# A four-layer graph network: layer 1's gathers started while layer 0's parts are stored, and its neighbours rearranged

## Chip, cores and metric

One core of a Trainium2 chip runs one program. The metric is the device time of one execution in microseconds. Its engines are TensorE (PE), VectorE (DVE), ScalarE (ACT), GpSimd (POOL) and SyncE (SP), each with an instruction queue of its own; they wait for each other with semaphores.

## The reference

12,500 nodes and 212,500 edges, 128 features. The edges are sorted by target (`dst`). Each of four layers sums over edges, updates the nodes, adds the old value and normalises:

```python
x = _layernorm(x + _L0_gnn_ref(x, W_t, W_u, b_u, src, dst))
x = _layernorm(x + _L1_gnn_ref(x, eps, stack([src, dst])))
x = _layernorm(x + _L2_gnn_ref(x, ew, ew, src, dst, eps, W1, b1, W2, b2))
x = _layernorm(x + _L3_gnn_ref(x, edge_attr, glob, W_e, b_e, eps, W1, b1, W2, b2, src, dst))
# L0: agg = segment_sum((x @ W_t)[dst], src) / deg;  relu(concat(x, agg) @ W_u + b_u)
# L1: agg = segment_sum(norm * x[dst], src);         agg + (1 + eps) * x
#     norm = deg_inv_sqrt[src] * deg_inv_sqrt[dst]
# L2: agg = segment_sum(x[src] * ew, dst);           relu(((1 + eps) * x + agg) @ W1 + b1) @ W2 + b2
# L3: agg = segment_sum(mish(x[src] + edge_attr @ W_e + b_e), dst); a two-layer network on it and glob
```

So layers 0 and 1 gather at the target and sum at the source, while layers 2 and 3 gather at the source and sum at the target.

## The kernel before

**Tiles and supertiles.** 128 nodes are a block (98 blocks), 128 edges a tile (1664 tiles, padding included), 128 tiles a supertile (13). Within a supertile the edges of layers 0 and 1 are sorted by source on the chip. The sums of all nodes stay in `acc`.

**Gathers.** GpSimd fetches a tile's 128 node rows with one indirect DMA into a ring `M` of 64 tiles: `gathers_src` (line 1765, issue on line 1786) in layers 0 and 1, `gathers_dst` (line 1798, issue on line 1821) in layers 2 and 3. In `gathers_src`, 8 gathers are a batch; before each batch beyond the first 8 GpSimd waits for `s_rel`. SyncE counts landed batches up on `s_arr` and releases slots on `s_rel` in `arrivals_src` (line 1832, waits on lines 1845, 1848 and 1851), five batches behind the arrivals. Layer 0 gathers from `in_x`, layer 1 from the table `t1` (the normalised nodes, scaled by the root of the inverse degree), layer 2 from `x2`, layer 3 from `t3`.

**The consumer.** TensorE multiplies one-hot matrices with gathered tiles, in steps; a supertile has 228 steps, in 38 units of 6. Two units are a group (`group_pe`, line 1717): it loads the group's table entries into registers (line 1702, `TENSOR_LOAD`), and for each unit clears two PSUM banks (1709, 1710), multiplies (1730), closes (1714) and yields. VectorE, in `unit_dve` (line 1745), adds the unit to `acc` (1754), yields, makes the one-hot matrices of the unit after the next (1736) and yields; every fourth unit it loads registers as well (1742).

**The sort** of supertile s+2 runs in slices beside layer 0's units of supertile s (`sort`, line 1201; `period` in `run_vector` and `run_tensor`). At each yield of `unit_dve` VectorE does one sort operation, and behind the unit what is left of the slice. TensorE does a slice after each unit. For each of 16 columns c of a supertile there are, in this order: rank matmuls on TensorE (1390, 1391), maxima of the positions on VectorE (1375, in slice `POS_AT`), masks on VectorE (1355, 1361, in slice `MASK_AT`), their scaling on ScalarE (1369), moves on TensorE (1399). Within a slice the masks stand ahead of the position maxima. The last two supertiles carry histograms of the degrees in the sort's place (1451, 1462).

**Node parts.** After each layer the nodes are updated in 25 parts of 4 blocks (`part`, line 1509). A part is a generator that each engine runs for itself; `ticks` starts one part a tick and advances the older ones first. In layer 0 a part is loaded by SyncE (1576), transposed, multiplied, normalised and stored in two DMAs (1660 to `x1`, 1662 to `t1`). It uses one of 6 buffers that lie over `M` and the sort's masks. In layer 1 a part is a sum of scaled `acc` and x (1601), a second sum (1603), the clearing of `acc` (1604), statistics (1639, 1640), a root on ScalarE (1642), reciprocal and product (1644, 1645) and the normalisation on ScalarE (1646).

**Between layers 0 and 1.** GpSimd waits for all stores of layer 0's parts before its first gather of layer 1. VectorE waits for them too, then has SyncE load the edge weights (2082) and two weight matrices, and makes with TensorE the tables for target order (`dst_tables`, line 1883) that layers 2 and 3 need: steps, positions and indices for all 1664 tiles. Only behind that does it start layer 1's units.

Of the kernel before, what the change touches and what calls it, by code (L numbers as in the profile page):

```python
# [4 lines left out]
P = 128  # L5
T = 128
# [10 lines left out]
SLOTS = 6  # L17
# [47 lines left out]
def graph_layers(nc, x_in, src_in, dst_in, edge_in, w_in, Wt, Wu, bu, eps1, eps2, W21, b21, W22, b22,  # L65
# [22 lines left out]
    with ExitStack() as ctx:  # L88
# [36 lines left out]
        s_late, s_srt, s_rel = (sem(n) for n in ("s_late", "s_srt", "s_rel"))  # L125
# [945 lines left out]
        def fast():  # L1071
# [11 lines left out]
            PART_W = [4 * 4 * P + 64, 8 * 4 * P + 64]  # L1083
            early = ExitStack()
# [24 lines left out]
            late.close()  # L1109
            third = ExitStack()  # L1110
# [3 lines left out]
            assert 6 * PART_W[0] <= RING * W1C + 3 * 16 * P  # L1114
# [25 lines left out]
            khi = sb("khi", [P, T], bf16)  # L1140
# [8 lines left out]
            posi = sb("posi", [P, 2, 8], i32)  # L1149
            lane8, tile8 = sb("lane8", [P, 2, 8], i32), sb("tile8", [P, 2, 8], i32)  # L1150
            lane_h, tile_f = sb("lane_h", [P, 2, 8], f16), sb("tile_f", [P, 2, 8])
# [47 lines left out]
            OP, SLICE = 0, 1  # L1199

            def sort(e, role, s, tv, tp, ta):
# [12 lines left out]
                for i in range(UNITS):  # L1214
# [134 lines left out]
                    for c in range(16):  # L1349
                        h, r = c % 2, c % 3  # L1350
# [22 lines left out]
                        if POS_AT[c] == i:  # L1373
                            for g in (2 * c, 2 * c + 1):
                                red[g] = v(lambda: e.tensor_reduce(
                                    posi[:, h, 4 * (g % 2):4 * (g % 2) + 4],
                                    group_ps(g).rearrange("p (b c) -> p c b", c=4), AX.X, ALU.max), rank[g],
                                    *([made[c - 2]] if c >= 2 else []), chain=False)
                                yield OP
                            v(lambda: e.tensor_scalar(tile8[:, h, :], posi[:, h, :], 7, 127, ALU.logical_shift_right, ALU.bitwise_and))  # L1380
                            v(lambda: e.tensor_scalar(lane8[:, h, :], posi[:, h, :], 127, None, ALU.bitwise_and), chain=False)
                            yield OP
                            v(lambda: e.tensor_copy(tile_f[:, h, :], tile8[:, h, :]))
                            lane_at[c] = v(lambda: e.tensor_copy(lane_h[:, h, :], lane8[:, h, :]), chain=False)
                            yield OP
# [379 lines left out]
            def gathers_src(e, layer, table):  # L1765
# [688 lines left out]
```

## Time and profile before

| | us |
|---|---|
| median of three runs | 9262.42 |
| lowest and highest | 9261.93, 9263.73 |
| profiled execution | 9272.82 |
| its span | 9270.6 |

The profiled execution is 0.1% longer than the median. The page's second section cuts the span into 40 slices of 232 us; each digit is the busy share of a slice in tenths:

```profile
PE   4778878878857666666643444444445777777776
DVE  6788888888775444444453222222224555555554
ACT  5445345351040000000012222222224777777775
POOL 2677777777437777777746777777776777777775
PEclk7888989987779777888766666666667888888887
```

Layer 0 fills slices 1 to 10, layer 1 lies in 12 to 20, layer 2 in 21 to 30 and layer 3 in the rest. The granted clock of TensorE is 0.788 of full speed over the whole.

### The profile page before, as it was taken

How to read it: one execution, taken by the hardware profiler on the slowest of the kernel's cores; microseconds unless marked ns; L12 is line 12 of the kernel's file. 1: busy time of each engine (PE TensorE's matmuls, PEld its weight loads, DVE VectorE, ACT ScalarE, POOL GpSimd, SP SyncE). 2: the span in 40 equal slices, each digit the busy share in tenths (PEclk: the TensorE clock that was granted, in tenths of full speed). 3: DMA queues.
4: the chain of work that ended last, by engine and by line, in shares of the span. 5: the costliest groups of instructions: out<-in, count | busy, mean ns of one | idle time of the engine just before them, and what ended most of it. 6: DMA issues, size and time to landing. Idle time of an engine off the chain costs nothing. (4 is left out here: it accounts for less than half of the span.)

```text
span 9270.6 us, 139621 instructions
## 1 busy us (share of the span) xinstructions
PE 6041.2 (65%) x35872; PEld 4960.3 (54%) x35873; DVE 4996.6 (54%) x10364; ACT 3294.3 (36%) x7312; POOL 6534.2 (70%) x6785
## 2 busy tenths in 40 slices
PE   4778878878857666666643444444445777777776
PEld 2556656657746555555532333333335666666665
DVE  6788888888775444444453222222224555555554
ACT  5445345351040000000012222222224777777775
POOL 2677777777437777777746777777776777777775
PEclk7888989987779777888766666666667888888887
DMA  1111111111132221222222222222223333333332
GB/s 31 39 51 50 50 51 50 50 50 49 34 105 53 53 53 53 53 53 53 53 71 63 63 63 60 63 63 60 63 63 84 107 108 109 108 109 107 108 105 76
DMA packets 572485, 623.52 MB, mean 67 GB/s; under 512 B 118766, under 2 KB 465050, under 8 KB 571802
## 3 DMA queue, kind: packets, MB, share of 16 engines
q0 software_dynamic: 212992, 436.63, 18.0%
q1 hardware_dynamic: 294120, 145.77, 5.5%
q10 hardware_dynamic: 64690, 32.10, 1.2%
q8 instruction: 417, 6.83, 0.3%
q14 instruction: 266, 2.18, 0.1%
HBM read 575.52 MB, written 38.51 MB: 66 GB/s over the span
## 5 line engine op out<-in xcount | busy, mean ns | idle before, releaser
L1730 PE MATMUL ps<-M,oh 128*128 x11856 | 2176.0, 336 | 580.7 <-SPq L1845 527.0
L1730 PEld LDWEIGHTS ps<-M,oh 128*128 128x128 f32 x11856 | 1957.6, 235 | 975.3 <-issue 816.4
L1786 POOL DMA_INDIRECT M<-in_x,ixb x1664 | 1691.7, 1017 | 588.3 <-issue 536.4
L1821 POOL DMA_INDIRECT M<-t,ixb x1664 | 1653.1, 993 | 504.2 <-issue 501.0
L1940 PE MATMUL ps<-M,oh 128*128 x7056 | 1284.3, 348 | 1084.1 <-ACT M L2256 1077.0
L1786 POOL DMA_INDIRECT M<-t,ixb x1664 | 1577.2, 948 | 512.5 <-issue 511.4
L1821 POOL DMA_INDIRECT M<-x,ixb x1664 | 1578.7, 949 | 504.1 <-issue 503.4
L1940 PEld LDWEIGHTS ps<-M,oh 128*128 128x128 f32 x7056 | 1192.3, 251 | 1254.9 <-issue 1182.2
L1754 DVE TENSOR_TENSOR acc<-acc,ps 128x774 f32 (+1 forms) x988 | 945.6, 957 | 1405.6 <-PE ps L1714 1361.4
L1956 DVE TENSOR_TENSOR acc<-acc,ps 128x1024 f32 x294 | 358.2, 1218 | 1603.3 <-PE ps L1714 1599.6
L2256 ACT ACTIVATE M<-M,wD 128x128 f32<-128x128 f32 x1664 | 517.2, 388 | 1488.8 <-DMA M<-x,ixb 1473.2
L1369 ACT ACTIVATE oht<-oneh,p1f 128x128 f16<-128x128 f16 x1664 | 644.6, 387 | 1083.7 <-DVE oneh L1355 1083.7
L1995 PE MATMUL ps<-we_sb,et 128*128 128x128 f32 x3328 | 590.0, 350 | 540.5 <-DVE vb L2032 512.4
L1736 DVE TENSOR_TENSOR oh<-ps,relS 128x768 f32<-128x768 f32 x992 | 942.1, 950 | 0.2
L1995 PEld LDWEIGHTS ps<-we_sb,et 128*128 128x128 f32 x3328 | 546.5, 257 | 562.4 <-issue 373.0
L1642 ACT ACTIVATE lay<-lay,eps_sb 128x4 f32<-128x4 f32 (+1 forms) x50 | 14.5, 290 | 2173.2 <-DVE lay L1640 2173.2
L1709 PE MATMUL ps<-ones_b,zwin 128*128 128x512 bf16 (+1 forms) x1282 | 543.1, 424 | 317.3 <-issue 153.9
L2040 DVE TENSOR_TENSOR M<-eb,vb 128x512 f32<-128x512 f32 x416 | 269.3, 689 | 715.6 <-ACT eb L2017 706.9
L1369 ACT ACTIVATE oht<-oneh,p2f 128x128 f16<-128x128 f16 x1664 | 642.3, 386 | 0.0
L1736 DVE TENSOR_TENSOR oh<-ps,relD 128x768 f32<-128x768 f32 x592 | 537.0, 948 | 0.0
L1710 PE MATMUL ps<-ones_b,zwin 128*128 128x472 bf16 (+2 forms) x1282 | 479.3, 374 | 0.0
L2013 ACT ACTIVATE eb<-eb 128x1024 f32<-128x1024 f32 x208 | 219.9, 1057 | 575.3 <-DVE eb L2035 575.3
(282 smaller groups left out, 7342.4 us busy)
## 6 DMA issues: line engine op xcount, KB each, us to landing
er<-in_edge_attr SPq DMA_DIRECT2D x414, 256.0 KB, 3.1
M<-t,ixb POOLq DMA_INDIRECT x3328
M<-in_x,ixb POOLq DMA_INDIRECT x1664
M<-x,ixb POOLq DMA_INDIRECT x1664
x<-lay SPq DMA_DIRECT2D x48, 256.0 KB, 2.3
part<-x ACTq DMA_DIRECT2D x48, 256.0 KB
lay<-in_x SPq DMA_DIRECT2D x24, 256.0 KB, 3.5
t<-lay SPq DMA_DIRECT2D x24, 256.0 KB, 3.0
```

What stands on the lines that cost most here:

```text
L1369: ins = e.activation(oht[:, r, k, w * P:(w + 1) * P], oneh[:, r, k, :], ACT.Copy, scale=pf[:, 8 * c + k:8 * c + k + 1])
L1709: e.matmul(ps[:, b0, 0:n0], zwin[:, 0:1].to_broadcast([P, P]), ones_b[:, 0:1].to_broadcast([P, n0]), start=True, stop=False)
L1710: e.matmul(ps[:, b0 + 1, 0:n1], zwin[:, 0:1].to_broadcast([P, P]), ones_b[:, 0:1].to_broadcast([P, n1]), start=True, stop=False)
L1730: ins = e.matmul(ps_flat[:, bass.ds(slot * pitch + b0 * 512, width)], oh[:, j, :], tile_at(M, tile, width), start=False, stop=False)
L1736: e.tensor_tensor(oh[:, u * US:u * US + US, :], ps[:, bank, 0:P].rearrange("p (a b) -> p a b", a=1).to_broadcast([P, US, P]), rel[:, k:k + ...
L1754: e.tensor_tensor(to, to, ps_flat[:, h * 1024:h * 1024 + US * pitch].rearrange("p (a b) -> p a b", b=pitch)[:, :, 0:width], ALU.add).then_ ...
L1786: e.indirect_dma_start(M[:, t % RING, 0:P], None, table[:, :], bass.IndirectOffsetOnAxis(ap=ixb[:, t:t + 1], axis=0)).then_inc(s_g[n % 16] ...
L1821: e.indirect_dma_start(M2[:, t % RING, :], None, table[:, :], bass.IndirectOffsetOnAxis(ap=ixb[:, t:t + 1], axis=0)).then_inc(s_g[n % 16], 16)
L1940: ins = e.matmul(ps_flat[:, bass.ds(slot * P, P)], oh[:, j, :], tile_at(M2, tile, P), start=False, stop=False)
L1956: e.tensor_tensor(to, to, ps_flat[:, 0:SPAN * P].rearrange("p (a b) -> p a b", b=P), ALU.add).then_inc(s_add, SG)
L1995: ins = e.matmul(ps[:, 5 + h, j * P:(j + 1) * P], et[:, h, j * P:(j + 1) * P], we_sb[:, :], start=True, stop=True)
L2256: ins = e.activation(M2[:, t % RING, :], M2[:, t % RING, :], ACT.Copy, scale=wD[:, t:t + 1])
```

## The change

1. **Gathers of layer 1 beside layer 0's parts.** The parts of layer 0 get 5 buffers of their own (`lay0`), which lie over the sort's masks and not over `M`. GpSimd waits, for each supertile, only for the parts that hold its rows (`rows_ready`).
2. **Tables in pieces.** `dst_tables` becomes a generator of 43 yields. VectorE and TensorE advance it by one piece every third unit of layer 1, from supertile 2 on. SyncE loads the weights for it after layer 1's first supertile.
3. **Layer 1's parts.** ScalarE multiplies x by 2 + eps (`twice`), VectorE adds scaled `acc` in one pass, and GpSimd clears `acc`.
4. **Sort.** The position maxima stand ahead of the masks in a slice, with three small buffers for two. `unit_dve` has one more yield between its addition and its one-hot matrices.
5. **TensorE's register load** for the next group stands right behind the closing of a group, ahead of the slice.

```diff
-SLOTS = 6
+SLOTS = 5
...
+            zeroth = ExitStack()
+            sb = place(zeroth)
+            sb("below0", [P, 2 * TILES + TILES + H + (SUP * KP + SG) // 2 + RING * W1C])
+            lay0 = sb("lay0", [P, SLOTS_OF[0] * PART_W[0]])
...
                 elif layer == 1:
-                    v(per_block(lambda k, c: e.scalar_tensor_tensor(a[:, c], acc[:, b0 + k, 0:P], dis[:, k:k + 1], x[:, c], ALU.mult, ALU.add)),
-                      loaded)
-                    v(lambda: e.scalar_tensor_tensor(z, x, eps_sb[:, 0:1], a, ALU.mult, ALU.add), stored)
-                    v(lambda: e.memset(sums, 0.0))
+                    act(lambda: e.activation(z, x, ACT.Copy, scale=twice[:, 0:1]), loaded, stored)
+                    v(per_block(lambda k, c: e.scalar_tensor_tensor(z[:, c], acc[:, b0 + k, 0:P], dis[:, k:k + 1], z[:, c], ALU.mult, ALU.add)),
+                      ta.at())
+                    if role == "g":
+                        wait(e, tv.at())
+                        e.memset(sums, 0.0).then_inc(s_z, 1)
...
             def group_pe(e, layer, regs, s, m):
...
-                at, ready = steps_pe(e, regs, 0, s * KP + m * SG)
+                if m == 0:
+                    load_pe(e, regs, 0, s * KP)
+                at, ready = steps_pe(e, regs)
...
                     close_pe(e, b0).then_inc(s_st, US)
+                    if h and m + 1 < KI:
+                        load_pe(e, regs, 0, s * KP + (m + 1) * SG)
                     yield
...
                 if layer:
                     e.wait_ge(s_ix, layer * (2 * SUP + 1))
+                    rows_ready(e, 0)
...
+            def last_part(s):
+                return min(int((s + 1) * T * NB * P / E + SPREAD), NB - 1) // 4
+
+            def rows_ready(e, s):
+                for i in range(SLOTS_OF[0]):
+                    n = len(range(i, last_part(s) + 1, SLOTS_OF[0]))
+                    if n:
+                        e.wait_ge(s_ns[i], 32 * n)
...
-                dst_tables(e, "v", tv, tp, ta)
...
+                pieces = dst_tables(e, "v", tv, tp, ta)
                 for s in range(SUP):
                     for u in range(UNITS):
-                        for _ in unit_dve(e, 1, regs, left, s, u):
-                            pass
+                        drain(unit_dve(e, 1, regs, left, s, u))
...
+                        if (s, u) == (PIECES_FROM, 0):
+                            e.wait_ge(s_ld, NLD + NLATE)
+                        if s >= PIECES_FROM and u % 3 == 0:
+                            next(pieces, None)
```

On GpSimd, from the end of layer 0's gathers to the first of layer 1, before (`s_ns` counts the stores of a buffer):

```order
L1786 DMA M<-in_x,ixb 128x128 x7
L1769 COPY ixb<-gS 128x64 [waits s_ns4,s_ns3,s_ns5,s_ns2,s_ix,s_ns1,s_ns0]
L1786 DMA M<-t,ixb 128x128 [waits s_ix,s_g14]
L1786 DMA M<-t,ixb 128x128 x7
L1786 DMA M<-t,ixb 128x128 [waits s_g15]
```

and now:

```order
L1807 DMA M<-in_x,ixb 128x128 x7
L1789 COPY ixb<-gS 128x64 [waits s_ns1,s_ns2,s_ns0,s_ix]
L1807 DMA M<-t,ixb 128x128 [waits s_ix,s_g14]
L1807 DMA M<-t,ixb 128x128 x7
L1807 DMA M<-t,ixb 128x128 [waits s_g15]
```

The wait has three buffers in it instead of six, and counts one part in each.

On ScalarE, in the steady course of layer 1's parts, before (`s_na` and `s_nv` are ScalarE's and VectorE's progress on a buffer, `s_nl` its loads):

```order
L1642 ACTIVATE lay01<-lay01,eps_sb 128x4 [waits s_na1,s_nv1]
L1646 ACTIVATE lay01<-lay01 128x128 [waits s_na1,s_nv1]
L1646 ACTIVATE lay01<-lay01 128x128 x3
L1642 ACTIVATE lay01<-lay01,eps_sb 128x4 [waits s_na2,s_nv2]
L1646 ACTIVATE lay01<-lay01 128x128 [waits s_na2,s_nv2]
```

and now:

```order
L1655 ACTIVATE lay01<-lay01,eps_sb 128x4 [waits s_na1,s_nv1]
L1659 ACTIVATE lay01<-lay01 128x128 [waits s_na1,s_nv1]
L1659 ACTIVATE lay01<-lay01 128x128 x3
L1612 ACTIVATE lay01<-lay01,twice 128x512 [waits s_na2,s_ns2,s_nl2]
L1655 ACTIVATE lay01<-lay01,eps_sb 128x4 [waits s_na2,s_nv2]
```

The product with `twice` for the next part stands behind the normalisation of the part before. VectorE's queue there was:

```order
L1645 SCALAR_TENSOR_TENSOR lay<-lay 128x4 [waits s_nv0]
L1601 SCALAR_TENSOR_TENSOR lay<-acc,degD,lay 128x128 [waits s_nv1,s_nl1]
L1601 SCALAR_TENSOR_TENSOR lay<-acc,degD,lay 128x128 x3
L1603 SCALAR_TENSOR_TENSOR lay<-lay,eps_sb 128x512 [waits s_nv1,s_ns1]
L1604 MEMSET acc 128x4x128 [waits s_nv1]
L1639 BN_STATS lay<-lay 128x6 [waits s_nv1]
```

and is now:

```order
L1658 SCALAR_TENSOR_TENSOR lay<-lay 128x4 [waits s_nv0]
L1613 SCALAR_TENSOR_TENSOR lay<-acc,degD,lay 128x128 [waits s_nv1,s_na1]
L1613 SCALAR_TENSOR_TENSOR lay<-acc,degD,lay 128x128 x3
L1652 BN_STATS lay<-lay 128x6 [waits s_nv1]
L1652 BN_STATS lay<-lay 128x6 x3
L1653 BN_AGGR lay<-lay 128x2 [waits s_nv1]
```

The sum now waits for ScalarE's product of its own part (`s_na1`), and the second sum and the clearing are gone.

On VectorE, in a unit of layer 0 that has both masks and maxima, before:

```order
L1754 TENSOR_TENSOR acc<-acc,ps 128x774
L1355 TENSOR_SCALAR oneh<-iota128b,tile_f 128x128 [waits s_p,s_v]
L1355 TENSOR_SCALAR oneh<-iota128b,tile_f 128x128
L1736 TENSOR_TENSOR oh<-ps,relS 128x768
L1355 TENSOR_SCALAR oneh<-iota128b,tile_f 128x128 x6
L1361 TENSOR_TENSOR ohl<-iota,lane_h 128x1024
L1375 TENSOR_REDUCE posi<-ps 128x4 [waits s_v,s_p] x2
L1380 TENSOR_SCALAR tile<-posi 128x8 [waits s_v]
```

and now:

```order
L1773 TENSOR_TENSOR acc<-acc,ps 128x774
L1360 TENSOR_REDUCE posi<-ps 128x4 [waits s_v,s_p] x2
L1755 TENSOR_TENSOR oh<-ps,relS 128x768
L1365 TENSOR_SCALAR tile<-posi 128x8 [waits s_v]
L1366 TENSOR_SCALAR lane<-posi 128x8
L1368 CAST tile_f<-tile 128x8 [waits s_v]
L1369 CAST lane_h<-lane 128x8
L1377 TENSOR_SCALAR oneh<-iota128b,tile_f 128x128 [waits s_p,s_v]
L1377 TENSOR_SCALAR oneh<-iota128b,tile_f 128x128 x7
L1383 TENSOR_TENSOR ohl<-iota,lane_h 128x1024
```

The two reductions moved from behind the masks to right behind the addition.

## Rows read from the trace of the kernel before

**Rows 1.** Page, section 1: busy time, share of the span and instructions of each engine.

```profile
PE 6041.2 (65%) x35872; PEld 4960.3 (54%) x35873; DVE 4996.6 (54%) x10364; ACT 3294.3 (36%) x7312; POOL 6534.2 (70%) x6785
```

**Rows 2.** Timeline of GpSimd: start, duration, instruction, idle time before and its releaser.

```profile
2674.28 0.23 POOL L1769 COPY ixb<-gS 128x64 int32<-128x64 int32 x1 [210.12 <-DMA t<-lay]
...
2766.51 0.95 POOL L1786 DMA_INDIRECT M<-t,ixb  x1 [8.68 <-issue]
...
4769.76 0.95 POOL L1786 DMA_INDIRECT M<-t,ixb  x1 [0.30 <-issue]
4904.93 0.23 POOL L1804 COPY ixb<-gD 128x64 int32<-128x64 int32 x1 [134.22 <-DMA x<-lay]
```

**Rows 3.** Groups, GpSimd, layer 0: busy us, mean ns, idle time before by releaser.

```profile
L1786 POOL DMA_INDIRECT M<-in_x,ixb x1664 | 1691.7, 1017 | 588.3 <-issue 536.4 <-SPq L1848 41.9 <-SPq L1851 9.7
```

**Rows 4.** Waits of GpSimd, 390 to 2151 us: total, times, longest.

```profile
POOL M L1786 <- SPq L1848: 17.8, 18, 5.1
```

**Rows 5.** Waits of VectorE in one supertile of layer 0, 1127 to 1298 us.

```profile
DVE acc L1754 <- PE ps L1714: 15.1, 12, 2.1
DVE acc L1754 <- issue: 6.3, 6, 1.1
```

**Rows 6.** Waits of VectorE in the same supertile's masks, 1159 to 1256 us.

```profile
DVE acc L1754 <- PE ps L1714: 1.4, 1, 1.4
```

**Rows 7.** Waits of TensorE, 1127 to 1298 us.

```profile
PE ps L1390 <- DVE posi L1375: 18.3, 9, 5.0
PE ps L1709 <- issue: 5.2, 8, 0.8
```

**Rows 8.** Timeline of SyncE's DMA issues, stores of layer 0's parts.

```profile
2570.65 0.51 SPq L1662 DMA_DIRECT2D t<-lay  x1
...
2672.30 0.47 SPq L1662 DMA_DIRECT2D t<-lay  x1
```

**Rows 9.** Page, section 6: issues of the second store, median us to landing.

```profile
t<-lay SPq DMA_DIRECT2D x24, 256.0 KB, 3.0
```

**Rows 10.** Timeline of VectorE, layer 1's first and eleventh additions.

```profile
2764.05 0.96 DVE L1754 TENSOR_TENSOR acc<-acc,ps 128x768 f32 x1 [2.79 <-PE ps L1714]
...
2794.09 0.95 DVE L1754 TENSOR_TENSOR acc<-acc,ps 128x768 f32 x1 [1.93 <-PE ps L1714]
```

**Rows 11.** Windows: length, busy us (x) of PE, PEld, DVE, ACT, POOL, clock, DMA, GB/s.

```profile
2543.00:2672.00 129.00, 85.18 (x588) 74.64 (x588) 107.49 (x469) 101.28 (x271) 0.00 (x0) 0.88 0.53 147
...
2764.00:4770.00 2006.00, 1364.44 (x7826) 1129.20 (x7824) 892.65 (x980) 0.00 (x0) 1519.43 (x1625) 0.81 0.20 53
4785.00:4903.00 118.00, 0.61 (x2) 0.11 (x2) 98.22 (x398) 47.84 (x123) 0.00 (x0) 0.51 0.39 108
```

**Rows 12.** Timeline of VectorE, one part of layer 1.

```profile
4852.57 1.14 DVE L1601 SCALAR_TENSOR_TENSOR lay<-acc,degD,lay 128x128 f32<-128x128 f32 x4
4853.81 0.75 DVE L1603 SCALAR_TENSOR_TENSOR lay<-lay,eps_sb 128x512 f32<-128x512 f32 x1
4854.74 0.48 DVE L1604 MEMSET acc<- 128x512 f32 x1 [0.17 <-DVE lay L1603]
4855.26 0.87 DVE L1639 BATCH_NORM_STATS2 lay<-lay 128x6 f32<-128x128 f32 x4
4856.16 0.38 DVE L1640 BATCH_NORM_AGGREGATE lay<-lay 128x2 f32<-128x6 f32 x4
4856.91 0.18 DVE L1644 RECIPROCAL lay<-lay 128x4 f32<-128x4 f32 x1 [0.36 <-ACT lay L1642]
```

**Rows 13.** Timeline of ScalarE, the normalisation of the part before.

```profile
4857.32 1.65 ACT L1646 ACTIVATE lay<-lay 128x128 f32<-128x128 f32 x4 [0.44 <-DVE lay L1645]
```

**Rows 14.** Groups by form, ScalarE, layer 0's parts.

```profile
L1589 ACT ACTIVATE lay<-ps 128x512 f32<-128x512 f32 x24 | 14.3, 597 | 10.4 <-PE ps L1554 9.6
```

**Rows 15.** Timeline of TensorE in a supertile with histograms, layer 0.

```profile
2203.30 0.37 PE L1709 MATMUL ps<-ones_b,zwin 128*128 128x471 bf16 x1 [0.59 <-DVE acc L1754]
```

**Rows 16.** Waits of TensorE's weight loads in the tables, 2675 to 2764 us.

```profile
PEld ps L1921 <- DVE seld L1920: 34.3, 18, 6.6
```

More of the change, by code:

```diff
@@ L1349, in sort @@
                     for c in range(16):
-                        h, r = c % 2, c % 3
+                        h = c % 3
+                        if POS_AT[c] == i:
+                            for g in (2 * c, 2 * c + 1):
+                                red[g] = v(lambda: e.tensor_reduce(
+                                    posi[:, h, 4 * (g % 2):4 * (g % 2) + 4],
+                                    group_ps(g).rearrange("p (b c) -> p c b", c=4), AX.X, ALU.max), rank[g],
+                                    *([made[c - 3]] if c >= 3 else []), chain=False)
+                                yield OP
+                            v(lambda: e.tensor_scalar(tile8[:, h, :], posi[:, h, :], 7, 127, ALU.logical_shift_right, ALU.bitwise_and))
+                            v(lambda: e.tensor_scalar(lane8[:, h, :], posi[:, h, :], 127, None, ALU.bitwise_and), chain=False)
+                            yield OP
+                            v(lambda: e.tensor_copy(tile_f[:, h, :], tile8[:, h, :]))
+                            lane_at[c] = v(lambda: e.tensor_copy(lane_h[:, h, :], lane8[:, h, :]), chain=False)
+                            yield OP
+                    for c in range(16):
+                        h, r = c % 3, c % 3
                         if MASK_AT[c] == i:
@@ L1514, in part @@
                 tl, ts, tv, tp, ta = tal[slot]
-                buf = part_bufs[layer // 2][slot]
+                buf = part_bufs[min(layer, 2)][slot]
                 x, a, aT, z = (buf[:, i * 4 * P:i * 4 * P + W] for i in range(4))
@@ L1520, in part @@
                 bank = ([2 * (j % 4), 2 * (j % 4) + 1], [], [4 + slot], [5 if j == len(PARTS) - 1 else 3])[layer]
-                used, stored = tv.at(), ts.at()
+                used, stored, read = tv.at(), ts.at(), ta.at()
                 sums = acc[:, b0:b0 + nb, 0:P]
@@ L1571, in part @@
                     wait(e, used)
+                    if layer == 1:
+                        wait(e, read)
                     if b0 + nb == NB and layer == 0:
@@ L1771, in supertile @@
                 def supertile(s, first):
+                    rows = table.shape[0] if layer == 0 else P * min(NB, 4 * (last_part(s) + 1))
                     for n in range(T // NQ):
@@ L1853, in arrivals_src @@
                 supertile(0, True)
+                if layer:
+                    late_loads(e)
                 for s in range(1, SUP):
@@ L2218, in run_tensor @@
                 all_parts(e, "p", 0, tal)
-                tv.inc(2)
-                e.wait_ge(s_ld, NLD + NLATE)
-                wait(e, tv.at())
-                dst_tables(e, "p", tv, tp, ta)
+                for t in tal:
+                    wait(e, t[2].at())
+                tv.inc(3)
+                pieces = dst_tables(e, "p", tv, tp, ta)
                 for s in range(SUP):
                     for m in range(KI):
-                        drain(group_pe(e, 1, regs, s, m))
+                        for h, _ in enumerate(group_pe(e, 1, regs, s, m)):
+                            if (s, m, h) == (PIECES_FROM, 0, 0):
+                                e.wait_ge(s_ld, NLD + NLATE)
+                            if s >= PIECES_FROM and (2 * m + h) % 3 == 1:
+                                next(pieces, None)
+                drain(pieces)
                 all_parts(e, "p", 1, tal)
```

96 lines of the change are left out of this document (50 added, 46 removed).

## The prediction

> **What bounds the kernel now.** The page's first section [rows 1] shows no engine near full: GpSimd 70%, TensorE 65%, VectorE 54%. GpSimd is the bound all the same. It issues 6656 gathers one behind the other; in layer 1 each takes 0.95 us with 0.30 us of "issue" behind it, which is no wait [rows 2]. From its index copy at 2674.28 to its last gather at 4769.76 are 2095 us for 1664 gathers, 1.26 us each, and the only gap of note is one of 8.68 us ahead of gather 64. So I read next what stands between the stretches of gathers: GpSimd is idle for 210.12 us between layers 0 and 1 and for 134.22 us between 1 and 2 [rows 2]. Both are what the change works on.
>
> Layer 0 is different. A gather there takes 1017 ns [rows 3], and GpSimd also waits for ring slots to be released, 17.8 us on line 1848 alone [rows 4]. The ring of 64 tiles is full, so the consumer sets the pace: TensorE multiplies a unit of 6 steps, VectorE adds it, and between units both do slices of the next supertile's sort. Who holds up VectorE is told by its waits in one supertile of 171 us: 15.1 us for TensorE and 6.3 us of its own register loads [rows 5]. In the 97 us in which the sort's masks are made, only 1.4 us of it are for TensorE [rows 6]. That stretch is VectorE's own work; the other waits lie in the light units, in which TensorE has no sort work between two groups.
>
> **The change, part by part.** The sum is made against the profiled execution, 9272.8 us (span 9270.6). It is 10.4 us above the median of 9262.4, and these 10.4 are taken off at the end.
>
> *Tables out of the way, gathers early.* Before, layer 1's consumer starts only after the tables: its first addition is at 2764.05 [rows 10], while the last store of layer 0's parts is issued at 2672.30 [rows 8]. The first 64 gathers fit in the ring and hid most of that, but the 1600 others came behind it. In the changed kernel GpSimd waits for parts 0 to 2 alone. Part 2's second store is issued at 2570.65 [rows 8] and lands 3.0 us later [rows 9]; 64 gathers then take 64 x 1.32 = 84 us at layer 0's pace (1017 ns and 0.30), so the ring is full near 2660. The consumer starts right behind the last store. SyncE's reading of the slot ends has no row here; I put it at 1.5 us, near the 1.1 us that VectorE's register load takes at most [rows 5]. TensorE's own start I put at 0.7 us and the first unit at 3.0, the pace of the first ten additions ((2794.09 - 2764.05) / 10 [rows 10]). So the first addition comes at 2672.8 + 1.5 + 0.7 + 3.0 = 2678, and not at 2764: 86 us. Gather 64 follows the first addition by 2.5 us in the rows, and does so again. **-86 us.** Bounds: -78, if the hand-overs take 8 us more; -88, if less.
>
> The tables' operations don't vanish. They are cut into 43 pieces, one every third unit from supertile 2 of layer 1 on. Before, they lay between the last store's landing at some 2675 and the first unit, 86 us with their loads, at most 2.0 us a piece. Layer 1's consumer needs 3.0 us a unit when it is free, and the gathers give it 128 x 1.26 / 38 = 4.24. Three units leave 3.7 us of cover for a piece; TensorE is idle for 32% of that stretch, VectorE for 56% [rows 11]. **0 us.**
>
> Five buffers in the place of six for layer 0's parts: the store of a part and the load that reuses its buffer stand next to each other in SyncE's queue, and the first write to the stored halves comes one part later, 129 / 25 = 5.2 us [rows 11], against 3.0 us for a store to land. **0 us.**
>
> *Layer 1's parts.* Before, a part takes 4.63 us: a chain on VectorE, from the scaled sum at 4852.57 over the reciprocal at 4856.91 to the next sum, with one small step of ScalarE in it (0.36 us) [rows 12]. ScalarE's normalisation of the part before, 1.65 us, runs beside it [rows 13]. The change takes the 0.75 us sum and the 0.48 us clearing off VectorE, to ScalarE and to GpSimd. But ScalarE's new step stands in its queue behind that normalisation, and VectorE's next sum waits for it. Now nothing runs beside anything: sum 1.14, statistics 0.87 and 0.38, square root 0.36 with its hand-over, reciprocal and product 0.36, normalisation 1.65, and the new step at 0.60, as a ScalarE copy of 128x512 takes in layer 0 [rows 14]; with three hand-overs of 0.05 that is 5.5 us. 25 x 0.87 = **+22 us**. Bounds: -36, if the new step ran ahead and VectorE kept its own 3.2 us alone; +30, if it takes 0.9 us.
>
> A rule of the Trainium skill speaks the other way. The page "Perfetto Trace Analysis", section "Optimizing Scalar/DVE Operations", says that if DVE is saturated, offloading some work to Scalar, or even GPSIMD, may make sense. VectorE is busy for 98.2 of 118 us here [rows 11], so the rule favours this move; by it the term would be -36. I go by the chain.
>
> *Position maxima first, register load ahead of the slice.* VectorE now reduces the positions right behind its addition, so that TensorE's rank matmuls, which waited 18.3 us a supertile for them [rows 7], get their turn earlier. A wait of TensorE costs nothing while VectorE is the bound; VectorE's own wait in that stretch is 1.4 us. Eleven supertiles carry a sort: 11 x 1.4 = 15 us. The register load of TensorE's next group shows as gaps of up to 0.8 us, 5.2 us a supertile [rows 7]. Most lie in light units, where nothing stands between two groups and the load stays where it is; I take 0.6 us a supertile: 7 us. In the last two supertiles, with histograms, TensorE does hold VectorE up, and the load leaves a gap of 0.59 us [rows 15]. Ahead of the 24 small matmuls it delays them by about as much; what is left is the address work now under them, half the gap, for 26 groups: 8 us. **-30 us.** Bounds: 0, and -104: VectorE's waits for TensorE would be more (11 x 15.1), but then the gathers bind, which can give their 17.8 us of waits and the ring's 86 us of lead.
>
> Sum: -86 + 22 - 30 = -94. 9272.8 - 94 = 9178.8, less 10.4 gives **9168 us**.
>
> **Rivals.**
> - *The offload pays*: VectorE's period in layer 1's parts falls to 3.2 us. For it: VectorE is the busy engine there. Against it: the chain above. 9168 - 58 = 9110.
> - *Layer 0 gains more*: TensorE's earlier ranks spread into the light units. For it: 13.7 us of waits there in each supertile. Against it: no sort matmul stands between those groups. In full 9168 - 74 = 9094, in half 9131.
> - *Layer 0's parts slow down*: stores and gathers now share the DMA engines (0.53 busy before [rows 11]). If a store lands 2 us after its buffer is wanted, each of 25 parts pays: 9168 + 50 = 9218.
> - *Slower than before*: the pieces hold up layer 1. TensorE's longest wait for VectorE in the tables was 6.6 us [rows 16]. A piece costs only what it takes beyond 3.7 us, so the change loses from 3.7 + 94 / 43 = 5.9 us a piece on; at 6.6 the time is 9168 + 43 x 2.9 = 9293. Against it: 2.0 us a piece at most.
>
> **How the numbers follow.** Chances: the forecast 0.68 (own range 9145 to 9192), offload 0.09, layer 0 in full or half 0.12, slower parts 0.07, slower than before 0.04. The range of 9105 to 9210 leaves out both slow cases, 0.11, and the full gain in layer 0, 0.05. A measurement tells 0.2%, 18.5 us, from no change: faster 0.94, same 0.02, slower 0.04.
>
> **What would show it.** Right: GpSimd's idle time between layers 0 and 1 splits into one stretch up to part 2's store and one of about 20 us ahead of gather 64; the last gather of layer 1 lies 116 us earlier, 86 by the consumer's start and 30 by layer 0; a part of layer 1 takes 5.5 us, with VectorE waiting for ScalarE in every one; VectorE's waits for TensorE in a sorted supertile fall from 15 to about 13 us. Wrong: further gaps among layer 1's gathers, a part of layer 0 above 5.5 us, or a sorted supertile at 167 us or below.

## The result, and the profile after

The changed kernel takes **9095.0 us** (median of 4 runs, 9090.4 to 9096.7) against 9262.2 for the kernel before on the same chip: a ratio of 0.982, 95% interval 0.980 to 0.984, 167 us less. The forecast was 9168, range 9105 to 9210. The direction was right and the forecast gain, 94 us, too small. The time lies below the range. One execution of the kernel before in e13 below took 15117 us at a granted clock of 0.447, the slower state, and is left out of every comparison.

The two profiled executions, of 9270.6 and 9088.6 us span, divide the 182 us between them like this. The borders are instructions of the traces; 15 of the 182 us are the distance of the two profiled executions from their medians, 10 above and 5 below.

| stretch (us) | before | after | difference | forecast |
|---|---|---|---|---|
| start to layer 0's last addition | 2536.8 | 2425.6 | -111.2 | -30 |
| to layer 1's first addition | 227.2 | 142.6 | -84.6 | -86 |
| to layer 1's last addition | 2020.7 | 2020.2 | -0.5 | 0 |
| to layer 2's first gather (parts) | 121.2 | 142.4 | +21.2 | +22 |
| layer 2 | 2128.1 | 2124.9 | -3.2 | 0 |
| layer 3 to the end | 2236.6 | 2232.9 | -3.7 | 0 |

Five of six rows are where they were put. All of the error is in the first.

GpSimd's timeline of the changed kernel, at the places of [rows 2]:

```profile
2462.59 0.23 POOL L1789 COPY ixb<-gS 128x64 int32<-128x64 int32 x1 [50.98 <-DMA t<-lay]
...
2570.87 0.94 POOL L1807 DMA_INDIRECT M<-t,ixb  x1 [26.62 <-issue]
...
4729.84 0.23 POOL L1837 COPY ixb<-gD 128x64 int32<-128x64 int32 x1 [4.05 <-DMA x<-lay]
```

The 210.12 us between layers 0 and 1 are now 50.98 us up to part 2's store and 26.62 us ahead of gather 64 (about 20 forecast; the 64 gathers took 81 us and not 84). The 4.05 us of the last row look like a gain on 134.22, but GpSimd now also clears a part's sums every 5.5 us, which cuts its wait into pieces.

VectorE's timeline, layer 1's first addition, answering [rows 10]:

```profile
2568.23 0.96 DVE L1773 TENSOR_TENSOR acc<-acc,ps 128x768 f32 x1 [6.01 <-PE ps L1729]
```

VectorE and then ScalarE in one part of layer 1, answering [rows 12] and [rows 13]:

```profile
4675.28 1.14 DVE L1613 SCALAR_TENSOR_TENSOR lay<-acc,degD,lay 128x128 f32<-128x128 f32 x4 [2.33 <-ACT lay L1612]
4676.46 0.87 DVE L1652 BATCH_NORM_STATS2 lay<-lay 128x6 f32<-128x128 f32 x4
4677.37 0.38 DVE L1653 BATCH_NORM_AGGREGATE lay<-lay 128x2 f32<-128x6 f32 x4
4678.11 0.18 DVE L1657 RECIPROCAL lay<-lay 128x4 f32<-128x4 f32 x1 [0.36 <-ACT lay L1655]
...
4680.81 1.14 DVE L1613 SCALAR_TENSOR_TENSOR lay<-acc,degD,lay 128x128 f32<-128x128 f32 x4 [2.33 <-ACT lay L1612]
```

```profile
4678.52 1.65 ACT L1659 ACTIVATE lay<-lay 128x128 f32<-128x128 f32 x4 [0.44 <-DVE lay L1658]
4680.07 0.71 ACT L1612 ACTIVATE lay<-lay,twice 128x512 f32<-128x512 f32 x1
```

From sum to sum are 5.53 us (5.5 forecast). VectorE waits 2.33 us for line 1612, and line 1612 starts behind the normalisation of the part before.

Waits of VectorE in one sorted supertile of the changed kernel (1084 to 1245 us, the 38 additions of the supertile, as in [rows 5]):

```profile
DVE acc L1773 <- PE ps L1729: 13.5, 11, 2.1
DVE acc L1773 <- issue: 2.5, 3, 1.1
```

The supertile takes 161.5 us in the place of 171. VectorE's waits for TensorE fell from 15.1 to 13.5, where the forecast had about 13, and none of them is left in the masks' stretch, where 1.4 us were. So the forecast's mechanism came, at its size. But 9.5 us of gain are six times as much. The "issue" waits fell as well, from 6.3 to 2.5, and one supertile varies. Supertiles 1 to 6 together, before (446 to 1470 us) and changed (440 to 1407.5 us):

```profile
DVE acc L1754 <- PE ps L1714: 102.9, 86, 2.1
DVE acc L1754 <- issue: 23.9, 33, 1.1
```

```profile
DVE acc L1773 <- PE ps L1729: 85.6, 70, 2.1
DVE acc L1773 <- issue: 7.9, 10, 1.1
```

Per supertile these are 17.2 and 4.0 us before, and 14.3 and 1.3 now, 5.5 of the 9.4 us that a supertile got shorter. The experiments began here.

### The profile page after: what moved, and what is told of

It reads as the page before. It is cut to its first block and busy times, and to the rows that moved or that the text cites. A ratio compares the mean times of both kernels' runs of the same rounds, so it can differ in the third digit from the quotient of the medians.

```text
span 9088.6 us, 139295 instructions
## 1 busy us (share of the span) xinstructions
PE 5886.2 (65%) x35522; PEld 4894.5 (54%) x35873; DVE 4931.7 (54%) x10315; ACT 3305.1 (36%) x7337; POOL 6542.4 (72%) x6810
## 5 line engine op out<-in xcount | busy, mean ns | idle before, releaser
L1747 PE MATMUL ps<-M,oh 128*128 x11856 | 2161.1, 331 | 595.0 <-SPq L1885 531.1
L1747 PEld LDWEIGHTS ps<-M,oh 128*128 128x128 f32 x11856 | 1918.3, 228 | 1003.4 <-issue 820.5
L1986 PE MATMUL ps<-M,oh 128*128 x7056 | 1262.1, 346 | 1109.3 <-ACT M L2310 1102.9
L1986 PEld LDWEIGHTS ps<-M,oh 128*128 128x128 f32 x7056 | 1179.7, 250 | 1267.9 <-issue 1205.4
L1724 PE MATMUL ps<-ones_b,zwin 128*128 128x471 bf16 (+1 forms) x932 | 381.6, 409 | 166.6 <-issue 117.6
```

What stands on the lines that cost most here:

```text
L1724: e.matmul(ps[:, b0, 0:n0], zwin[:, 0:1].to_broadcast([P, P]), ones_b[:, 0:1].to_broadcast([P, n0]), start=True, stop=False)
L1747: ins = e.matmul(ps_flat[:, bass.ds(slot * pitch + b0 * 512, width)], oh[:, j, :], tile_at(M, tile, width), start=False, stop=False)
L1986: ins = e.matmul(ps_flat[:, bass.ds(slot * P, P)], oh[:, j, :], tile_at(M2, tile, P), start=False, stop=False)
```

## Experiments on layer 0

Theory A: the order helps VectorE itself, by giving its register load a cover, that is, work that runs while the load does. Theory B: the move of TensorE's register load is what helps. Four kernels, all made from the kernel before, ran on one chip, on which the kernel before took 9268.9 us (8 runs).

**e1: position work first, with three buffers and the additional slot step.** The position block moves as a whole; nothing else of the change is in it.

```diff
-                        h, r = c % 2, c % 3
+                        h = c % 3
+                        if POS_AT[c] == i:
...
+                    for c in range(16):
+                        h, r = c % 3, c % 3
                         if MASK_AT[c] == i:
...
-                        if POS_AT[c] == i:
...
+                yield
                 yield
                 batch(e, h, relS, k0 + 2 * US, 6)
```

> The kernel before with the position work placed ahead of the masks in a slot (three buffers for it, and the slot step behind the addition), nothing else changed. Theory A (the order gives VectorE's own register load a cover: in the trace before, its load of about 1 us stands behind four small casts and ends 1.1 us late, six times a supertile; now eight masks and the lane compare stand behind the last wait): VectorE's 'issue' waits in a sorted supertile fall from 6.3 to about 2.5 us, a sorted supertile takes 161 to 163 us in the place of 170.7, the last addition of layer 0 comes 75 to 105 us earlier, time 9160 to 9190. Theory B (the gain in the changed kernel comes from TensorE's register load having moved): a sorted supertile stays at 168 to 170 us, time 9230 to 9250.

Measured: 9181.4 us, ratio 0.990 (0.989 to 0.992), as theory A had it. Supertiles 1 to 6 take 161.2 us each in the place of 170.8 and layer 0's last addition comes at 2451.2, 85.6 us earlier. Supertiles 11 and 12 stay at 199.5 and 183.2 (200.2 and 185.3 before).

**e2: the same without the additional slot step.**

> As the run before this one, but without the additional slot step behind the addition: the one-hot batch again comes after the first of the two reductions. Theory A: the batch's place is of no matter, within 10 us of the kernel with the step; a sorted supertile 161 to 163 us. Rival: the step, which lets both reductions run ahead of the batch and so gives TensorE its ranks 0.9 us earlier, carries the gain: a sorted supertile at 166 us or above, 50 us more than with it.

Measured: 9193.5 us, 0.992 (0.990 to 0.994); 163.3 us a sorted supertile, last addition at 2460.7. The order gives 76 us and the step 10 more. Both figures lie just outside what theory A had (163.3 for 161 to 163; 12 us between the medians for 10) and far from its rival's (166, and 50 us), so the order carries the gain.

**e3: TensorE's register load behind the last matmul of its group, alone.**

```diff
...
                 close_pe(e, b0).then_inc(s_st, US)
+                if h and m + 1 < KI:
+                    load_pe(e, regs, 0, s * KP + (m + 1) * SG)
                 yield
```

> The kernel before with TensorE's register load behind the last matmul of a group, nothing else. Theory A: VectorE does not wait for TensorE in the masks' stretch, so little comes of it: a sorted supertile 169.5 to 170.7 us; in the two supertiles with histograms, where TensorE holds VectorE up, 200.2 and 185.2 us fall by 3 to 9 us each; time 9245 to 9260. Theory B: a sorted supertile at 166 us or below, time below 9215.

Measured: 9231.1 us, 0.996 (0.995 to 0.997), below what theory A had for it. A sorted supertile takes 170.2 us, so B falls for these. But supertiles 11 and 12 fall by 17.8 and 17.6 us, where I had written 3 to 9 each. The windows of those two supertiles, of the kernel before and of e3 (length, then busy us of PE, PEld, DVE, ACT and POOL, granted clock, DMA share, GB/s):

```profile
2151.40:2351.60 200.20, 172.83 (x1506) 152.53 (x1505) 160.25 (x336) 0.00 (x0) 152.69 (x147) 0.74 0.18 49
2351.60:2536.80 185.20, 161.49 (x1362) 140.98 (x1360) 144.84 (x296) 0.00 (x0) 72.15 (x70) 0.74 0.10 26
```

```profile
2149.60:2332.00 182.40, 159.82 (x1505) 143.58 (x1504) 159.30 (x335) 0.00 (x0) 144.59 (x128) 0.80 0.17 46
2332.00:2499.70 167.70, 146.64 (x1362) 131.70 (x1360) 144.72 (x296) 0.00 (x0) 99.11 (x88) 0.82 0.14 36
```

The number of matmuls is the same within one record, and TensorE is busy 27.9 us less with them (334.3 and 306.5), at a granted clock of 0.80 and 0.82 instead of 0.74. Only 7 of the 35 us are idle time of TensorE. So with the loads moved, TensorE ran more of its work at the higher clock level. Whether the smaller gaps raised the clock was not tried by itself.

**e4: VectorE's register load alone**, issued under its fourth addition in the old order of the slots.

```diff
-                if u % 4 == 0:
+                if u == 0:
                     blocks_dve(e, regs, left, 32, s * UNITS + u, min(4, UNITS - u), US)
...
                                 ALU.add).then_inc(s_add, US)
+                if u % 4 == 3 and u + 1 < UNITS:
+                    blocks_dve(e, regs, left, 32, s * UNITS + u + 1, min(4, UNITS - u - 1), US)
                 yield
```

> The kernel before with VectorE's load of its next four block numbers issued right behind its fourth addition, so that it runs under the addition; the slot's order is left as it was. This measures VectorE's register load by itself. Theory A: 'issue' waits of VectorE fall from 6.3 to below 1.5 us, a sorted supertile takes 165 to 166 us, 9 or 10 loads are also covered in supertiles 11 and 12, time 9195 to 9215. Theory B: the wait turns into one for TensorE, a sorted supertile at 169 us or above, time above 9240.

Measured: 9229.5 us, 0.996 (0.994 to 0.997), between what A and B had. So is a sorted supertile at 167.6 us. Its waits, supertiles 1 to 6 (442.5 to 1447.4 us):

```profile
DVE acc L1754 <- PE ps L1714: 105.6, 88, 2.5
```

The "issue" waits ahead of additions are gone, 4.0 us a supertile, and 3.1 us of that reach the supertile; the waits for TensorE rise from 17.2 to 17.6. So the register load by itself accounts for a third of the 9.6 us of e1. In the masks' stretch, moreover, VectorE still waits for TensorE here (2.8 us in one supertile) and does not in e1: the order takes away both.

**What else the order does** can be read in one unit. VectorE in the kernel before, the end of a unit with a register load:

```profile
1229.91 1.02 DVE L1375 TENSOR_REDUCE posi<-ps 128x4 int32<-128x392 f32 x2
1230.97 0.17 DVE L1380 TENSOR_SCALAR tile<-posi 128x8 int32<-128x8 int32 x1
1231.05 0.17 DVE L1381 TENSOR_SCALAR lane<-posi 128x8 int32<-128x8 int32 x1
1231.25 0.17 DVE L1383 CAST tile_f<-tile 128x8 f32<-128x8 int32 x1
1231.33 0.16 DVE L1384 CAST lane_h<-lane 128x8 f16<-128x8 int32 x1
1232.61 0.96 DVE L1754 TENSOR_TENSOR acc<-acc,ps 128x774 f32 x1 [1.11 <-issue]
```

and in the changed kernel, the same unit:

```profile
1177.95 1.02 DVE L1360 TENSOR_REDUCE posi<-ps 128x4 int32<-128x392 f32 x2
1178.90 0.94 DVE L1755 TENSOR_TENSOR oh<-ps,relS 128x768 f32<-128x768 f32 x1
...
1180.11 0.16 DVE L1369 CAST lane_h<-lane 128x8 f16<-128x8 int32 x1
1180.18 1.62 DVE L1377 TENSOR_SCALAR oneh<-iota128b,tile_f 128x128 f16<-128x128 bf16 x8
1181.48 0.68 DVE L1383 TENSOR_TENSOR ohl<-iota,lane_h 128x1024 f16<-128x1024 f16 x1
1182.08 0.95 DVE L1773 TENSOR_TENSOR acc<-acc,ps 128x774 f32 x1
```

Before, the unit's last waits for semaphores stood among four small steps of 0.17 us. Whatever the queue had to do ahead of the next addition (the register load of 0.97 us, which the trace has at 1231.27, the semaphores, the address) came behind it and showed. Now eight masks and the lane compare, 2 us of work with no wait between them, stand there, and the addition starts 0.60 us after the compare, while that is still running. Over supertiles 1 to 6, before and e1, per supertile: idle time ahead of additions falls from 21.2 to 15.7 us (e4 has 17.7), of which 2.9 us were waits for TensorE and 2.6 "issue"; idle time ahead of the position work falls from 1.5 to 0.2, and VectorE's busy time, in which overlapping instructions count once, from 146.3 to 143.2. These make up the 9.6 us within 0.3. The last item is no wait at all: the same instructions, whose single times still add up to 174 us, lined up so that neighbours overlap.

**The pieces do not add.** e1 and e3 bring the last addition 85.6 and 37.1 us earlier, 122.7 together; the changed kernel has 111.2. Of the 11.5 us that are missing, 10 lie in the last supertile: it takes 175.7 us, against 183.2 in e1 and 167.7 in e3. VectorE gains 9.4 us a supertile on the gathers until it has caught up. The addition trails its gather by 66 us at supertile 1, by 20 at supertile 8 and by 19 from then on, and supertiles 8 to 10 take 165 to 168 us, the pace of 128 gathers of 1001 ns and 0.30 us. In the last supertile a gather takes 1.14 us, and the changed kernel, unlike e3, has no lead left to hide that. Waits of GpSimd in the changed kernel (390 to 2100 us), answering [rows 4]:

```profile
POOL ixb L1789 <- SPq L1888: 1.0, 1, 1.0
POOL M L1807 <- SPq L1891: 0.9, 3, 0.3
```

The 17.8 us of waits on released slots are gone. In its first eight supertiles layer 0 is bound by VectorE, in 8 to 10 and in the last by GpSimd's gathers.

## Experiments on the other terms

Each is made from the changed kernel. **e5** takes the layer-0 edits back (the diffs above, the other way round), and with them the same early load of TensorE in layers 2 and 3, which e3 did not have. **e6** puts layer 1's sum, scaled sum and clearing back on VectorE. **e7** issues ScalarE's product a step earlier and gives the parts a fifth buffer, which was not tried alone:

```diff
-            SLOTS_OF = [SLOTS, 4, 2, 2]
+            SLOTS_OF = [SLOTS, 5, 2, 2]
...
                     act(lambda: e.activation(z, x, ACT.Copy, scale=twice[:, 0:1]), loaded, stored)
+                    yield
```

**e8** is e7 with e4's load.

> The changed kernel with its layer-0 edits taken back (masks ahead of the position work, two buffers, no additional slot step, TensorE's load at the head of its group); early gathers, tables in pieces and layer 1's parts stay. If the terms add: a sorted supertile 170.5 to 171 us, the first addition of layer 1 comes 142 to 144 us after the last one of layer 0 (227 before), a part of layer 1 takes 5.5 us, so 84.7 less and 22 more: 62 below the kernel before, 9197 to 9207. Rival (part of the change's gain came from the layers acting on each other, the consumer's lag among them): above 9220 or below 9185.

> The changed kernel with layer 1's parts as before: sum, scaled sum and clearing all on VectorE. By the chain (ScalarE's product stands behind the normalisation of the part before, so nothing runs side by side): a part takes 4.63 us again, GpSimd's idle time between layers 1 and 2 goes from 156 back to 134 us, 22 us less than the changed kernel: 9067 to 9079. By the rule that offloading a busy VectorE pays: the same or slower than the changed kernel, 9095 or more.

> The changed kernel with one more step in layer 1's parts, so that ScalarE's product for the next part is issued ahead of the normalisation of the part before, and five buffers instead of four. By the chain: VectorE keeps only its own 3.2 us (sum 1.14, statistics 0.87 and 0.38, 0.36 for the square root, reciprocal and product 0.36, hand-overs); a part takes 3.2 to 3.4 us, 25 x 2.2 = 55 us less than the changed kernel: 9032 to 9048. Rival (the stores and loads of a part, 512 KB in 3.2 us, or GpSimd's clearing on VectorE's shared port set the pace): 4 us a part or more, 9055 or more.

> The kernel of the run before this one, with VectorE's load of four block numbers issued right behind its fourth addition as well. If the position work's new place already covers that load (theory A): a sorted supertile of layer 0 (the second to the seventh, before the gathers bind) 160 to 161.5 us, time within 6 us of that kernel. If the load's 3.4 us and the order's 9.4 us are separate: 158 us a sorted supertile there; the time still moves little, since the gathers bind from then on, but VectorE's waits for the gathers' arrivals start a supertile or two earlier.

They ran on another chip, on which the kernel before takes 11690 us. The same kernels ran again as **e9** to **e12**, on one more chip of this kind, with 11688 us:

> The same kernel as e5 on another chip, since on the one of e5 to e8 the DMAs landed later and the kernel before took 11690 us. If the terms add: a sorted supertile 170.5 to 171 us, first addition of layer 1 142 to 144 us after the last of layer 0, a part of layer 1 5.5 us, and 0.9932 of the kernel before (62 us less). Rival (a part of the change's gain came from the layers acting on each other): a ratio above 0.996 or below 0.991.

> The same kernel as e6 on this chip. Its part period was 4.63 us there, as forecast; so 22 us less than the changed kernel, 0.9795 of the kernel before. Rival (GpSimd, SyncE or the next layer's start takes it back): 0.9815 or above.

> The same kernel as e7 on this chip. Its part period was 3.43 us there: 25 x 2.1 = 52 us less than the changed kernel, 0.9763 of the kernel before. Rival: the shorter stretch ends later at the next layer's gathers, whose stores land last: 0.978 or above.

> The same kernel as e8 on this chip. If the order already covers VectorE's load: a sorted supertile of layer 0 before the gathers bind 160 to 161.5 us, time within 6 us of e11. If the load's 3.4 us come on top: 158 us a supertile there, and 0 to 10 us less than e11, since the gathers bind sooner.

So **e13** and **e14** took traces of the kernel before and of the changed one on such a chip (11683 us), with **e15** and **e16** beside them, and **e17** and **e18** repeated these two on a fourth (11694 us). The times and ratios that the expectations give for a chip like the first could not come on these.

> The kernel before, for its trace on this chip. Where the gathers land as on the first chip: 9262 us, a sorted supertile 170.7 us, 227 us between the last addition of layer 0 and the first of layer 1. Where they land later, as in e5 to e12: 11690 us, a sorted supertile 220 to 228 us, set by the gathers, and 300 us between the two additions (8.0 us a part and the tables' 86), against the 216 of e5 to e12.

> The changed kernel on the same chip. Where the gathers land as on the first chip: 0.982 of the kernel before. Where they land later: layer 0 waits for gathers and not for VectorE, so its edits give little there (0 to 30 us), the early start gives 86, layer 1's parts take 22: 11600 to 11640, a ratio of 0.992 to 0.996.

> The changed kernel with its layer-0 edits taken back. Where the gathers land as on the first chip: if the terms add, 62 us less than the kernel before, ratio 0.993; otherwise above 0.996 or below 0.991. Where they land later: 11700 to 11720 as in e5 and e9; then either the early start's 86 us are given back inside layer 1 (its 2640 us longer than the kernel before's), or they never came (the two additions no closer than before).

> The changed kernel with ScalarE's product issued ahead of the normalisation of the part before. Where the gathers land as on the first chip: a part 3.43 us, 52 us less than the changed kernel, ratio 0.976, the fastest of all. Where they land later: again 3.43 us and 52 us less than the changed kernel, ratio 0.988.

> As e15. Where the gathers land as on the first chip: layer 0's parts 4.8 us each, first addition of layer 1 142 to 144 us after the last of layer 0, a part of layer 1 5.5 us, ratio 0.993 (62 us less than before) if the terms add; above 0.996 or below 0.991 if not. Where they land later: parts of layer 0 8.0 us, ratio 1.000 to 1.004.

> As e16. Where the gathers land as on the first chip: a part of layer 1 3.43 us, ratio 0.976, 52 us less than the changed kernel. Where they land later: ratio 0.988.

| kernel | us | ratio to before (95%) |
|---|---|---|
| before itself, e13 | 11704.9 | 1.002 (1.000 to 1.003) |
| changed, e14 | 11612.3 | 0.992 (0.989 to 0.995) |
| layer 0 undone, e5, e9, e15, e17 | 11722, 11710, 11728, 11721 | 1.003, 1.001, 1.004, 1.003 |
| layer 1's parts undone, e6, e10 | 11574, 11575 | 0.991, 0.990 (0.987 to 0.994) |
| product ahead, e7, e11, e16, e18 | 11568, 11563, 11557, 11562 | 0.990, 0.988, 0.988, 0.989 (0.985 to 0.993) |
| product ahead and VectorE's load, e8, e12 | 11568, 11558 | 0.989, 0.988 |

e14 came out where I had put it for such chips (11600 to 11640), but by other terms: the layer-0 edits gave 43 us for 0 to 30, and the early start 43 for 86, since before it the two additions lay 259 us apart and not 300. The stretches of the table above, in profiled executions on these chips:

| stretch (us) | before, e13 | changed, e14 | layer 0 undone, e15 | parts undone, e10 | ahead, e16 |
|---|---|---|---|---|---|
| to layer 0's last addition | 3267.5 | 3224.8 | 3261.4 | 3214.9 | 3206.6 |
| to layer 1's first | 259.1 | 216.1 | 215.4 | 216.3 | 215.2 |
| to layer 1's last | 2622.3 | 2636.6 | 2638.0 | 2659.0 | 2644.8 |
| parts | 121.0 | 142.2 | 142.3 | 121.2 | 92.4 |
| layer 2 | 2563.1 | 2568.9 | 2552.6 | 2564.9 | 2564.6 |
| layer 3 to the end | 2869.3 | 2828.9 | 2880.1 | 2831.6 | 2859.3 |

**Layer 1's parts.** The time from part to part is 5.52 us changed, 4.63 undone and 3.43 with the product ahead (3.2 to 3.4 expected), on every chip that ran them. The stretch follows: 142, 121, 92 us. VectorE and ScalarE in e11, with the product ahead:

```profile
6153.83 1.14 DVE L1614 SCALAR_TENSOR_TENSOR lay<-acc,degD,lay 128x128 f32<-128x128 f32 x4 [0.24 <-ACT lay L1612]
```

```profile
6153.09 0.70 ACT L1612 ACTIVATE lay<-lay,twice 128x512 f32<-128x512 f32 x1
6153.70 1.63 ACT L1660 ACTIVATE lay<-lay 128x128 f32<-128x128 f32 x4
```

Same instructions as in the changed kernel, but the product stands ahead of the normalisation, and VectorE waits 0.24 us for it instead of 2.33. e14 and e16, on one chip, differ by 55.6 us in their medians, where 52 were expected; the executions of either scatter by 40 to 70 us. On a chip like the first, 9095 less the 50 us of stretch would be 9045 us: an estimate, not a run. On whole times the 22 us of e6 and e10 lie within the intervals' width, and e7 and e11 are only 5 and 12 us below e6 and e10 where the stretch has 29, so the stretch decides and not the ratio. Offloading costs 21 us as the change has it, and saves 29 with the product a step earlier. The Trainium skill's rule that offloading a saturated DVE may make sense (page "Perfetto Trace Analysis", section "Optimizing Scalar/DVE Operations") holds or fails here by a place in a queue.

**The early start gave 43 us here, not 85.** GpSimd, ScalarE and the issues of SyncE's stores in e14, in layer 0's parts:

```profile
3262.76 0.97 POOL L1807 DMA_INDIRECT M<-t,ixb  x1 [0.77 <-POOL ixb L1789]
...
3341.95 0.94 POOL L1807 DMA_INDIRECT M<-t,ixb  x1 [0.31 <-issue]
3444.07 0.94 POOL L1807 DMA_INDIRECT M<-t,ixb  x1 [101.17 <-issue]
```

```profile
3276.26 0.28 ACT L1655 ACTIVATE lay<-lay,eps_sb 128x4 f32<-128x4 f32 x1
3324.94 0.60 ACT L1598 ACTIVATE lay<-ps 128x512 f32<-128x512 f32 x1 [48.40 <-remote]
```

```profile
3276.84 0.51 SPq L1675 DMA_DIRECT2D t<-lay  x1
...
3340.06 0.51 SPq L1675 DMA_DIRECT2D t<-lay  x1
```

The 64 gathers are issued from 3262.8 to 3342. In nearly that time the parts all but stop: from one part's store to the next are 63 us, and ScalarE and VectorE are idle for 48.40 and 36.05 us on end. From the first part's store to the last's are 185.1 us, against 109.7 in e13, so the stall costs 75 us. It stands in the same place in e5 to e12 and e15 to e18, and is not in e13, which has no gathers there. In the changed kernel on the first chip the longest distance from store to store was 5.5 us, as before the change.

It is not the loads and stores that fail to move. What the DMA queues carried (packets, MB; q0 has the gathers) from 3262.8 to 3282 us, and from 3282 to 3338 us:

```profile
q1 hardware_dynamic: 4752, 2.36, 43.2%
q0 software_dynamic: 448, 0.92, 19.7%
```

```profile
q0 software_dynamic: 1440, 2.95, 20.2%
```

The queue of the loads and stores (q1) moved 2.36 MB up to 3282, which is all of the nine transfers issued by then, and then stood empty. VectorE's wait has no releaser in the trace, only "issue":

```profile
3313.04 0.69 DVE L1608 TENSOR_TENSOR lay<-ps,bias 128x512 f32<-128x512 f32 x1 [36.05 <-issue]
```

ScalarE's says "remote", which names nobody either, and many semaphore records are missing in that time. So the stall goes with the gathers, and what it waits for is open. My rival "layer 0's parts slow down", priced at 50 us, had the place but not the mechanism, which was stores that land late in each of 25 parts. The kernel before needs 32 us more on these chips too between the same two additions (259.1 against 227.2), so 43 us of the gain are left.

**Layer 0** is not bound by VectorE here: a supertile takes 217 to 238 us, of which VectorE is busy for 144, and the addition comes 92 to 114 us behind its gather in both kernels. That it waits for gathers to land is the likely reading; the trace names no releaser for most of these waits. The layer's edits give 42.7 us in the traces (36.6 from e15 to e14) in the place of 111. So e8 and e12 could not show whether VectorE's own load is worth more on top of the new order: no supertile was VectorE's, and both ended within 5 us of e7 and e11.

**Layer 3** is the row where e14 and e15 differ most, by 51 us. In the 14 profiled executions on these chips it takes 2813 to 2859 us in the nine that load TensorE's registers behind a group (e6 to e8, e10 to e12, e14, e16, e18) and 2864 to 2903 in the five that load them at its head (e5, e9, e13, e15, e17): 42 us between the means. In layer 3 that load is the only difference of order between e14 and e15. On the first chip the change gave 3.7 us there.

**Whether the terms add** on a chip like the first one stayed untested in whole kernels; there the stretches of the one trace add up to its total. On the other four the version without the layer-0 edits is slower than the kernel before by 22 to 45 us in its medians of 10 runs, and in three of four the interval lies above 1. The stretches of e15 sum to 13 us less than e13's, but its profiled execution is the second fastest of its ten, 36 us below their median. So the early start's 43 us are lost again there, 21 of them in layer 1's parts; where the rest goes the single traces do not settle.

## Where the prediction was right and where it failed

- **Early start, -86:** right, -84.6. The hand-overs I put at 1.5, 0.7 and 3.0 us held in sum. On the other chips it was 43.
- **Tables in pieces, 0:** right, 0.5 us on 2020. The rival in which they hold up layer 1 did not occur.
- **Five buffers, 0:** right on the first chip, with 5.5 us at most from store to store, as before.
- **Layer 1's parts, +22:** right, +21.2. The product took 0.71 us and not 0.60.
- **Layer 0, -30 with a bound of -104:** wrong, -111.2, beyond the bound. This is the step that failed, in three places.
  - I took VectorE's waits for TensorE in the masks as all that the new order could give, 11 x 1.4 us. They went, as forecast. But [rows 5] had its own register loads beside them, 6.3 us a supertile, and I put them at nothing, though the diff's order is what decides what stands in front of them. Nor did I look at overlap, which no row of waits shows. Measured: 9.4 us a supertile, and of e1's 9.6 some 2.9 are waits for TensorE, 2.6 the loads' "issue" time, 1.3 idle time between small steps and 3.1 overlap.
  - TensorE's load I took at 7 us in the sorted supertiles, where e3 has 3, and at 8 in the last two, where it gives 35. Of 0.59 us of gap I credited half, to 26 groups. There are 38, each gave 0.93 us, and four fifths of that is busy time at a higher granted clock. The row of the 0.59 us names VectorE's addition as releaser, not the load.
  - The bound of -104 came from the gathers' 17.8 us of waits and the ring's 86 us of lead. The lead was indeed used up (the lag fell from 66 to 19 us), but the bound gave nothing to the first supertile (9.4 us shorter) and too little to the last two (27 us shorter together).
  - My own sign of being wrong came: a sorted supertile at 167 us or below. It takes 161.
- **The rival "layer 0 gains more"** had the sign and, at 9094, almost the number, by a wrong mechanism: TensorE's ranks spreading into light units. The waits for TensorE that went are mostly those in the masks' stretch, and 14.3 us of 17.2 stayed. That the number fits is chance.
- **The range** left out 5 in 100 at its low end for the full gain of layer 0. With the register loads as a term of their own, 11 x 3.8 us by [rows 5], the sum would have been near 9126, inside the range and still 31 us too high.

## What to carry to other kernels

Ask of a reordering what stands behind each engine's last wait before its critical instruction: work without waits there covers register loads, semaphores and addresses and lets neighbours overlap, and small dependent steps there cover nothing. Price an engine's own "issue" gaps as a term, beside its waits for others. Compare waits over several periods, with windows cut at the same instruction: one wait more or less at an edge was 2 us here. An offload pays or costs by its place in the other engine's queue, and work run beside a burst of gathers can stop for nearly as long as they are issued, on one chip and not on another.

## What the runs showed of the hardware that was not expected

- Moving TensorE's register load forward in its queue, 38 times, went with a granted clock of 0.80 to 0.82 instead of 0.74 and 27.9 us less busy time over some 2870 matmuls. Of the 35 us only 7 were idle time of TensorE.
- Chips differ more than the change does. On two chips the kernel before took 9262 and 9269 us, on the others 11683 to 11694. VectorE's instructions take the same time on both kinds (a part of layer 1 is 4.63 us); the gathers move 54 GB/s in layer 1 on the first and 41 on the others, and layer 0's parts stop beside 64 gathers on the others alone. Why is not shown by any run. The windows of layer 1 in the changed kernel, first chip and e14:

```profile
2570.00:4580.00 2010.00, 1354.06 (x7761) 1128.36 (x7889) 932.36 (x1113) 0.00 (x0) 1519.66 (x1625) 0.82 0.21 54
```

```profile
3460.00:6070.00 2610.00, 1586.33 (x7713) 1203.96 (x7842) 918.24 (x1106) 0.00 (x0) 1509.83 (x1613) 0.70 0.16 41
```

A change can so be worth 1.8% on the one kind and 0.8% on the other, with the same instructions.
